# A gated cross-attention layer: query and key stages put into one block, feed-forward weights kept on chip, residual with bias formed in the query stage

## The reference, cut to what matters

```
q = layernorm(x) @ Wq + bq            # 2048 rows, 16 heads of 32
k, v = split(ctx @ Wkv + bkv)         # 4096 keys
q, k, v rounded to 8-bit steps; softmax(q k^T) rounded; out = probs @ v
x = x + tanh(g_xattn) * (out @ Wp + bp)
w1, w2 rounded to (-1, 0, 1) * mean|w|
h = layer_norm(gelu(silu(w1 . round(rmsnorm(layernorm(x))) + b1)))
x = x + tanh(g_ffn) * (w2 . round(rmsnorm(h)) + b2)
```

## Time and profile before

| | |
|---|---|
| median of the runs | 1780.82 us (1779.55 to 1785.1, 3 runs) |
| the profiled execution, its own time | 1781.48 us |
| span from its first to its last instruction | 1779.7 us |
| mean granted TensorE clock | 0.962 |
| busy: PE, DVE, ACT, POOL | 87%, 92%, 78%, 74% of the span |
| query stage, from the first instruction to the last rounding | 0 to 82 us |
| key stage, from the first transpose to the last store's issue | 91.6 to 259.7 us |
| attention begins | 262.4 us |

### The profile page before, as it was taken

One profiled execution on the slowest core, in us unless ns is written; L12 is line 12 of the kernel. 1 busy time (PEld: TensorE's weight loads), 2 busy tenths in 40 slices (PEclk: granted clock), 3 DMA queues, 4 the chain that ended last, 5 costly groups with the idle time before them and its releaser, 6 DMA issues.

```text
span 1779.7 us, 34673 instructions
## 1 busy us (share of the span) xinstructions
PE 1541.5 (87%) x13207; PEld 754.3 (42%) x13207; DVE 1636.9 (92%) x2214; ACT 1393.1 (78%) x1351; POOL 1320.5 (74%) x1297
## 2 busy tenths in 40 slices
PE   7799967898888889889898988988888887789996
PEld 4344422444444444444444444444444443333332
DVE  7869968999999999999999999999999998388987
ACT  4468867788898888889888888987888886577873
POOL 0156755899889889898988898898999898355342
PEclk9989987999999999999999999999999998799998
DMA  6769966999958999995898998688888876123223
GB/s 207 258 200 356 340 245 128 169 179 175 171 106 149 170 171 186 169 162 111 148 179 170 184 170 151 115 149 160 148 158 141 156 141 132 60 46 85 63 63 83
DMA packets 725640, 282.62 MB, mean 159 GB/s; under 512 B 676121, under 2 KB 680793, under 8 KB 724194
## 3 DMA queue, kind: packets, MB, share of 16 engines
q1 hardware_dynamic: 724098, 277.47, 75.5%
q0 software_dynamic: 704, 1.62, 0.3%
q10 hardware_dynamic: 672, 1.31, 0.2%
HBM read 76.59 MB, written 35.95 MB: 63 GB/s over the span
## 4 chain that ended last, share of the span: by engine, by line
DVE 40%; POOL 18%; PE 14%; issue 10%; ACT 2%; DMA 1%; POOLq 0%; SPq 0%; DVEq 0%; ACTq 0%
DVE att_scaled L1662 38%; POOL att_probsT L1395 14%; PE att_scores L1181 3%; PE att_scores L1121 2%; PE att_ps_o L1201 2%; PE att_scores L1141 2%; POOL att_low_row L1385 2%; PE att_scores L1182 1%; POOL att_bias_row L1388 1%; PE att_scores L1083 1%; ACT att_pairs L1261 1%; DVE att_v_largest L1631 1%; PE att_ps_v L1111 0%; ACT att_head_area L1293 0%; PE att_ps_o L1102 0%
## 5 line engine op out<-in xcount | busy, mean ns | idle before, releaser
L1662 DVE TENSOR_SCALAR_CACHE_REDUCE att_scaled<-att_scores,layer_nsq 128x1536 f32<-128x1536 f32 (+1 forms) x768 | 1202.0, 1634 | 19.7 <-PE att_scores L1141 16.6
L1261 ACT ACTIVATE att_pairs<-att_scaled,att_bias_row 128x4096 uint8<-128x4096 f32 x256 | 950.5, 3713 | 112.2 <-DMA att_pairsT<-att_pairs 76.9
L1395 POOL CAST att_probsT<-att_pairsT 128x2048 bf16<-128x2048 uint8 x512 | 953.6, 1891 | 101.9 <-DMA att_pairsT<-att_pairs 90.3
L1141 PE MATMUL att_scores<-first_head_area 96*128 96x512 bf16 x1024 | 299.3, 397 | 94.7 <-DVE att_scaled L1662 78.4
L1141 PE MATMUL att_scores<-att_head_area 96*128 96x512 bf16 x1024 | 290.2, 386 | 64.2 <-DVE att_scaled L1662 60.7
L1102 PEld LDWEIGHTS att_ps_o<-att_v_head,att_probsT 128*128 128x128 bf16 x8192 | 243.1, 96 | 65.9 <-issue 3.6
L1102 PE MATMUL att_ps_o<-att_v_head,att_probsT 128*128 128x32 bf16 x8192 | 245.3, 177 | 2.7 <-DMA att_v_head<-layer_w2T 2.6
L1141 PEld LDWEIGHTS att_scores<-first_head_area 96*128 96x128 bf16 x1024 | 81.8, 99 | 256.7 <-DVE att_scaled L1662 173.0
L1083 PE MATMUL att_scores<-att_head_area 96*128 96x512 bf16 x621 | 170.6, 384 | 0.0
L1141 PEld LDWEIGHTS att_scores<-att_head_area 96*128 96x128 bf16 x1024 | 80.0, 98 | 212.9 <-DVE att_scaled L1662 149.6
L1083 PE MATMUL att_scores<-first_head_area 96*128 96x512 bf16 x570 | 158.7, 388 | 0.0
(11 more groups left out here) (181 smaller groups left out, 1630.6 us busy)
## 6 DMA issues: line engine op xcount, KB each, us to landing
layer_w2T<-ctx_T SPq DMA_DIRECT2D x96, 256.0 KB, 3.9
k_rows<-kv_parts SPq DMA_DIRECT2D x32, 392.0 KB, 4.3
q_w_in<-in_L_ffn_w_dram SPq DMA_DIRECT2D x32, 256.0 KB, 2.8
kv_weights_ctx_in<-in_ctx_dram SPq DMA_DIRECT2D x32, 256.0 KB, 4.8
kv_weights_w_in<-in_L_ffn_w_dram SPq DMA_DIRECT2D x32, 256.0 KB, 5.1
ctx_T<-kv_inT SPq DMA_DIRECT2D x8, 1024.0 KB, 6.5
q_x_in<-in_x_dram SPq DMA_DIRECT2D x16, 256.0 KB, 3.6
terns<-kv_tern SPq DMA_DIRECT2D x32, 128.0 KB, 4.7
```

The costliest lines, as they stand in the source:

```text
L1141: last = pe.matmul(buffer[:, x:x + 512], q_head[slot][:, at:at + P], k_head[slot][:, STARTS[j] + x:STARTS[j] + x + 512], start=True, stop= ...
L1261: act.activation(pairs[g % R_BUFS][:, :].bitcast(U8).rearrange("p (c two) -> p two c", two=2), scaled[u][:, :].rearrange("p (two c) -> p t ...
L1395: pool.tensor_copy(probsT[g % C_BUFS][:, parity * HALF:(parity + 1) * HALF, :].rearrange("p k q -> p (k q)"), bytes_now.rearrange("p (n tw ...
L1662: dve.tensor_scalar(scaled[u][:, STARTS[j]:STARTS[j] + WIDTHS[j]], scores[(g * NCH + j) % 2][:, 0:WIDTHS[j]], kept["nsq"][:, g:g + 1], Non ...
```

## The change

Both projections become one function, `project`, in one block. What moves and what goes:

- **One block.** PE, ACT and DVE run `query_step(g)` for the row tiles and then `step(g)` for the context tiles, PE and ACT with the last query steps between the first three key steps. SP's `next_loads` is followed by bv, the last four `xb` stores and the last query stores; ctx tile 4 and all later loads come behind these.
- **Weights.** The 32 pieces are loaded once into 32 places of SBUF (w2T's area, a part of `o_sum`, a new area). ACT sums them as before; `round_weights(m)` rounds in place, three steps behind instead of one, in `tern` buffers that are part of `q_stage`, so the first waits for the query stores.
- **Residual with bias.** POOL adds the gated bias to each x tile that the query stage has loaded anyway (`add_bias`), into `xb` buffers in `o_sum`, and SP stores it. x's buffers are free again only after both DVE and POOL have used them. `inT` lies in the same part of `o_sum`, so ACT's first copy into it waits for all `xb` stores.
- **Gates first.** ACT issues the gate loads ahead of wq and takes the Tanh before the first square root; bp's load follows bq.
- POOL's order: bias adds with two groups of query stores between them, b1's split, the third group, then the pads and the partition sum. `wq` shares its place with the key parts.
- The last block of values is kept and its largest taken two steps earlier.

```diff
-def project_queries(nc, t, kept, next_loads):
-def project_keys_values(nc, t, kept, wk, bk, wv, bp, gates, weights_in, ...):
+def project(nc, t, kept, o_sum, next_loads, wk, bk, wv, bp, gates, weights_in, ...):
...
+        shared = c.sb("shared", [P, PART_BUFS * KEY_ROW // 2], F32)
+        wq = shared[:, 0:CT * C].rearrange("p (k n) -> p k n", n=C)
+        parts = [shared[:, i * KEY_ROW // 2:(i + 1) * KEY_ROW // 2].bitcast(BF16) for i in range(PART_BUFS)]
+        inT = [o_sum[:, i * CT * BLOCK:(i + 1) * CT * BLOCK].rearrange("p (k n) -> p k n", n=BLOCK) for i in range(2)]
+        tern = [q_stage[:, 0, i * C:(i + 1) * C] for i in range(TERN_BUFS)]
+        xb = [o_sum[:, i * C:(i + 1) * C] for i in range(XB_BUFS)]
...
+                def load_x(g):
+                    after(sp, xn_ready, g - X_BUFS + 1)
+                    after(sp, xb_ready, g - X_BUFS + 1)
+                    sp.dma_start(x_in[g % X_BUFS][:, :], x_tiles[:, g, :]).then_inc(x_loaded[g % X_BUFS], 16)
+                def load_pieces(g):
+                    after(sp, w_summed, 2 * (g - 1))
+                    for m in (2 * g, 2 * g + 1):
+                        sp.dma_start(pieces[m], tile_and_piece(t, m)[1]).then_inc(a_loaded[g % 2], 16)
...
-                        after(sp, tern_ready, n - IN_BUFS + 1)
-                        sp.dma_start(w_in[n % IN_BUFS][:, :], piece).then_inc(w_loaded[n % IN_BUFS], 16)
-                    m = g - 2
+                    m = g - ROUND_LAG - 1
...
+                for g in range(X_BUFS, QT):
+                    load_x(g)
+                    store_x(g - X_BUFS)
+                    load_pieces(g - 2)
+                for g in range(QT - 2, QT):
+                    load_pieces(g)
+                for buffer, source, sem in next_loads:
+                    sp.dma_start(buffer, source).then_inc(sem, 16)
                 sp.dma_start(kept["bv"][:, :], t["L0_xattn_bkv"][C:2 * C].rearrange("(k p) -> p k", p=P),
+                for i in range(QT - X_BUFS, QT):
+                    store_x(i)
+                store_queries(sp, 3, last_q_stored)
                 for g in range(STEPS + 1):
+                    if g == 4:
+                        sp.wait_ge(q_stored, 16 * 3 * (H // 4))
+                        sp.wait_ge(last_q_stored, 16 * (H // 4))
+                        for a in range(3):
+                            sp.dma_start(q_first[a * D:(a + 1) * D, :], t["q_ints"][0, :, :]).then_inc(q_loaded, 16)
                     step(g)
...
+                        if n < 2:
+                            pe.wait_ge(weights_in, 64)
+                            pe.wait_ge(q_math, QPER * (QT - 2 + n) + 1)
...
+                pe.wait_ge(q_const, 1)
+                for g in range(Q_FULL):
+                    query_step(g)
+                for g in range(3):
+                    step(g)
+                    query_step(Q_FULL + g)
+                for g in range(3, STEPS):
                     step(g)
...
                 def round_weights(m):
+                    if m == 0:
+                        act.wait_ge(w_math, 2)
+                        act.wait_ge(q_stored, 16 * 3 * (H // 4))
+                        act.wait_ge(last_q_stored, 16 * (H // 4))
+                    act.activation(pieces[m], pieces[m], ACT.Identity,
...
+                        if g == 0:
+                            for i in range(XB_BUFS):
+                                act.wait_ge(xb_stored[i], 16 * QT // XB_BUFS)
...
+                    if live(g - ROUND_LAG, KT - 1):
+                        round_weights(g - ROUND_LAG)
...
+                    if g - ROUND_LAG == KT - 1:
+                        round_weights(KT - 1)
+                for i, name in enumerate(("g_xattn", "g_ffn")):
+                    act.dma_start(gates[:, i:i + 1], t[name].partition_broadcast(P)).then_inc(gates_in, 16)
+                act.dma_start(wq, t["L0_xattn_Wq"].rearrange("(k p) n -> p k n", p=P)).then_inc(q_weights_in, 16)
+                act.dma_start(bq[:, :], t["L0_xattn_bq"].partition_broadcast(P)).then_inc(q_weights_in, 16)
+                act.dma_start(bp[:, :], t["L0_xattn_bp"].partition_broadcast(P)).then_inc(gated_ready, 16)
+                act.wait_ge(gates_in, 32)
+                act.activation(kept["gate_tanh"][:, :], gates[:, :], ACT.Tanh).then_inc(gates_ready, 1)
...
+                def add_bias(i):
+                    pool.wait_ge(x_loaded[i % X_BUFS], 16 * (i // X_BUFS + 1))
+                    after(pool, xb_stored[i % XB_BUFS], 16 * (i // XB_BUFS))
+                    pool.tensor_tensor(xb[i % XB_BUFS], x_in[i % X_BUFS][:, :], bp[:, :], ALU.add).then_inc(xb_ready, 1)
+                for i in range(QT):
+                    add_bias(i)
+                    if i in STORE_AT:
+                        store_queries(pool, STORE_AT.index(i), q_stored)
                 split_bias()
+                store_queries(pool, 2, q_stored)
+                pool.wait_ge(q_ready, QT)
+                pool.wait_ge(w_summed, 2 * QT)
+                for i in range(PART_BUFS):
+                    pool.memset(parts[i][:, H * HEAD_PITCH:KEY_ROW], 0.0).then_inc(pads_ready, 1)
+                pool.wait_ge(total_ready, 1)
+                pool.partition_all_reduce(total_all[:, :], total[:, :], P, RADD).then_inc(total_all_ready, 1)
```

More of the change, by code:

```diff
@@ L473, in project_keys_values @@
         q_loaded = c.sem("q_loaded")
-        xb_loaded = [c.sem(f"xb_loaded{i}") for i in range(XB_BUFS)]
         xb_stored = [c.sem(f"xb_stored{i}") for i in range(XB_BUFS)]
@@ L478, in project_keys_values, with store_queries @@
         gated_ready = c.sem("gated_ready")
-        NPER = 5
-        K_STORES = 2
+        QPER, W_LAG = 6, 2
+        NPER, K_STORES = 5, 2
         PER_BLOCK = BLOCK // P
         STEPS = KT + 5
-        XB_LOAD, XB_ADD, XB_STORE = 2, 4, 6
+        ROUND_LAG = 3
+        Q_FULL = QT + 2
+        Q_HEADS = 48
+        STORE_AT = (10, 14)
         x_tiles = t["x"].rearrange("b (i p) c -> p (b i) c", p=P)
         xb_tiles = t["xb"].rearrange("b (i p) c -> p (b i) c", p=P)
-        def row_tile(g, first):
-            i = (g - first) // 2
-            return i if (g - first) % 2 == 0 and 0 <= i < QT else None
+        sq_tiles = sq[:, :].rearrange("p (h i) -> p h i", i=QT)
+        def store_queries(eng, i, stored):
+            eng.wait_ge(q_kept, (i + 1) * QT // 4)
+            rows = slice(i * ROWS // 4, (i + 1) * ROWS // 4)
+            for g in range(H // 4):
+                eng.dma_start(t["q_ints"][4 * g:4 * g + 4, :, rows].rearrange("h d r -> (h d) r"),
+                              q_stage[:, g, rows]).then_inc(stored, 16)
         with nc.Block() as block:
@@ L582, in step @@
                             last.then_inc(v_ready, 1)
-                for g in range(STEPS):
+                pe.wait_ge(q_const, 1)
[5 more added lines that the diff above has]
+                for g in range(3, STEPS):
                     step(g)
@@ L598, in round_weights @@
                     after(act, tern_stored[m % TERN_BUFS], 16 * (m // TERN_BUFS))
-                    act.activation(tern[m % TERN_BUFS][:, :], w_in[n][:, :], ACT.Sign, bias=up_down[:, 1:2]).then_inc(tern_ready, 1)
+                    act.activation(tern[m % TERN_BUFS], pieces[m], ACT.Sign, bias=up_down[:, 1:2]).then_inc(tern_ready, 1)
                 def keep_values(j):
@@ L1755, in gated_layer @@
             ctx_in = [kv.sb(f"ctx_in{i}", [P, C], F32) for i in range(IN_BUFS)]
-            w_in = [kv.sb(f"w_in{i}", [P, C], F32) for i in range(IN_BUFS)]
             kv_loaded = kv.sem("loaded")
```

508 lines of the change are left out of this document (220 added, 288 removed).

## The result

| | before | after |
|---|---|---|
| median of the runs (five each, one chip) | 1779.55 us | 1788.39 us (1786.82 to 1790.25) |
| ratio after / before, 95% interval | | 1.0046 [1.0033, 1.0060] |
| last query products begin | 74.27 | 86.66 |
| key products of tile 0, of tile 3 | 94.29, 109.07 | 100.69, 117.28 |
| first scores of attention | 262.47 | 269.21 |

The time lies in the predicted range (1773 to 1791), 5.4 us above the point forecast of 1783. It is 8.8 us more than before, and so slower by more than the 5.3 us that count as no change: the outcome to which the prediction gave 0.29, where it gave 0.53 to no change. The time that rival 3 gave was 1793.

What follows compares the result with a forecast made beforehand. The query stage was taken as bound by DVE and PE, the key stage by PE. On 1781.5: + 4.5 (DVE held) - 2.4 (hole) - 1.0 (tail) + 1.3 (Exp table) = 1783.9, said as 1783 us; range 1773 to 1791.

Steps and rivals of the forecast that it cites:

- rival 3: Query stage: DVE pays each bias add in full, + 13.9 for + 4.5, giving 1793 us; chance 0.16.
- DVE held by the adds: Query stage: ten POOL adds each hold DVE 0.45 us, + 4.5 us, bounds 0 and 13.9.
- hole, last query products to key 3: Between query and key stage: key 3 at 106.7 for 109.07, gain 2.4 us, bounds 0 and 15.3.
- key stage, product 3 to 31: Key stage: bound by PE without stalls, so fewer loads and adds there are worth nothing.
- tail, product 31 to attention: End of key stage: k_rows leaves at 258.2 for 258.63, xb store behind it gone; 1.0 us gained, between 0 and 2.
- Exp's table load: Attention's start: Exp needs its own table after Sqrt's, + 1.3 us on the path, 0 if PE's wait has another cause.
- An add starts when its x tile lands: Query step: add starts 1.35 us after L320, ends at 2.6, so L338 is held 0.65 us.
- The feedback: Query stage: a held step makes the next add come earlier in its step; two holds sum to some 0.65 us.
- Its own range: The forecast's own range: 1779 to 1788 us, from a hold of 0.1 to 0.85, 2 us either way at the hole.
- rival 1: Hole: the clock stays up, gain 6.8 us, giving 1779, or 1774.5 with adds that hold nothing; chance 0.22.
- rival 2: Hole: xb stores land early and the block runs through, gain 15.3 us, giving 1771; chance 0.12.
- rival 4: Query stage's start: POOL's first arithmetic stalls 7.21 us, + 4.5 us, giving 1788; chance 0.08.

Runs made afterwards that it cites:

- e8: The kernel before, run again unchanged for a second profile: 1776.83 us, one run.
- e1: Kernel after with each bias add cut to 16 of 512 columns; order, waits, loads and stores stay: 1776.57 us, ratio 0.9982 to before.
- e2: Kernel after with whole adds, from the fifth on also waiting for the rounding of five tiles back: 1779.57 us, ratio 1.0000 to before.
- e3: Kernel after with eight xb buffers instead of four, so no add waits for the xb store of four tiles back: 1785.96 us, ratio 1.0032.
- e4: Kernel after with the xb buffers in the first head's area, so inT no longer waits for xb stores: 1782.86 us, ratio 1.0025 to before.
- e7: e6 with SP issuing context tiles 4 and 5 ahead of the last query stores: 1763.90 us, ratio 0.9904 to before.
- e10: Kernel after with the bias adds put back into the key stage, x tiles loaded a second time: 1774.13 us, ratio 0.9962 to before.
- e6: e5 with key weights, context tiles and value weights loaded within the query loop, key products not awaiting value weights: 1770.87 us, ratio 0.9931 to before.
- e9: e7 with the key weights loaded as four 256 KB slices from row tile 5 on: 1764.14 us, ratio 0.9914 to before.
- e11: Kernel after with POOL's two groups of query stores behind all sixteen adds: 1785.80 us, ratio 1.0038 to before.
- e5: Kernel after with the edits of e2 and e4 together: 1770.14 us, ratio 0.9928 to before.

## Why the prediction was nearly right, and which step was not

| term of the sum | forecast | measured in after |
|---|---|---|
| DVE held by the adds | + 4.5 (0 to 13.9) | + 12.4 (86.66 - 74.27) |
| hole, last query products to key 3 | - 2.4 | - 4.2 (34.80 to 30.62) |
| key stage, product 3 to 31 | 0 | 0.0 (132.03 both) |
| tail, product 31 to attention | - 1.0 | - 1.5 (21.37 to 19.90) |
| Exp's table load | + 1.3 | 0 |

The first four give + 6.7, and attention began 6.74 later. The two profiled spans differ by 8.7, the medians by 8.8: the other 2 us lie behind the start of attention, where e8 and the first profile of the same kernel differ by 2.3.

**The step that failed** is the size of the hold, and in it the sentence "An add starts when its x tile lands", 1.35 us after L320. The mechanism and its place were right (L338 to L359, exempt what reads PSUM, rival 3's point of decision at a mean hold of 0.75; measured 12.4 over ten steps, 1.24). But these are the waits of POOL in after, us in total, times, longest:

```profile
POOL layer_o_sum L585 <- DMA xb<-layer_o_sum: 29.7, 10, 5.2
```

Ten adds start only when the xb store of four tiles back has landed, and SP issues that store 0.4 us behind the x tile's load:

```profile
40.09 0.38 SPq L303 DMA_DIRECT2D pre_x_in<-in_x_dram  x1
40.52 0.43 SPq L312 DMA_DIRECT2D xb<-layer_o_sum  x1
...
44.77 1.26 POOL L585 TENSOR_TENSOR layer_o_sum<-pre_x_in,layer_bp 128x512 f32<-128x512 f32 x1 [3.67 <-DMA xb<-layer_o_sum]
```

In the four steps from 27 to 48 us the adds begin 1.85 to 2.55 us after L627, about where the part that can be held begins (1.97), and each holds it for 0.97 to 1.05 us. The two that come sooner (1.60 and 1.17) hold 0.75 and 0.31. The wait stands in the diff (`after(pool, xb_stored[i % XB_BUFS], ...)`); the prediction's walk has no such wait, and priced the stores at 0.12 us a step, as what makes landings later. e1 shows the price of the adds (11.8 us), e2 that the moment alone decides it (8.8 with whole adds), e3 that the store's landing is only part of the lateness.

The feedback on which the prediction counted is there: the load and the store of 40.09 and 40.52 go out while L651 is held (39.92), so that the longer step brings the next add sooner in its own. In e1, where nothing is held, the same four adds begin 2.92 to 3.65 us after the bias add, in after 0.8 to 1.6 us sooner. By the prediction's working, from a start at 1.35, that halves the hold; from where the adds really start it doesn't take them out of the part that is held.

Rival 3 is what happened, with six holds near its price and two of twice that. Above their usual lengths the eight held instructions add 9.7 us. Two shorter holds (0.92 and 0.48 us for 0.17, at 56.18 and 61.08) add 1.1, and 0.74 is a wait of DVE for PE at 63.94: PE had been idle for 2.57 us, its granted clock was 0.50 from 58 to 60, and eight matmuls took 4.92 us. The last 0.9 I haven't placed.

**Luck.** The range held, but not by the sum. Its own range allowed a hold of 0.1 to 0.85 us. With 12.4 for 4.5 and the other terms as forecast it would have given 1791.8, less the 0.7 between profile and median 1791.1, just outside. Hole, tail and table load each came out better than forecast, 3.6 us together, and the range had been stretched into rival 3.

**The hole**: right in its cause and order. Key 0 began 14.0 us after the last query products (forecast some 13), behind the xb stores on SP's queue, over 6 us long at half the clock; context tile 4 made PE wait 1.72. The rows of after:

```profile
87.52 5.84 SPq L312 DMA_DIRECT2D xb<-layer_o_sum  x4
...
100.69 6.18 PE L426 MATMUL pre_ps_k<-kv_weights_wk,layer_o_sum 128*128 128x512 f32 x8 [7.90 <-ACT layer_o_sum L509]
...
116.79 0.66 PE L412 MATMUL pre_ps_in<-layer_ident,kv_weights_ctx_in 128*128 128x128 f32 x4 [1.72 <-DMA kv_weights_ctx_in<-in_ctx_dram]
```

e4 and e7 take the two waits away one by one. Key product 1 began 6.7 us after product 0 where I had priced 8.1, as the clock came back earlier (0.57 from 104 to 106, 1.00 from 106 to 108), and PE's wait for context tile 4 was 1.72 for some 3; so the gain was 4.2.

**Fewer loads and adds in the key stage: nothing.** Right, by the 132.03 us of before, after and e10 from key product 3 to 31.

**The Exp's table load** cost nothing. It didn't stand behind the wait for POOL's row but ran under it. Rows of after:

```profile
273.90 1.28 ACT L1258 ACT_TABLE_LOAD   x1
276.27 3.71 ACT L1258 ACTIVATE att_pairs<-att_scaled,att_bias_row 128x4096 uint8<-128x4096 f32 x1 [1.08 <-POOL att_bias_row L1385]
```

The Exp begins 7.06 us after attention's start, 7.05 in before; ACT's idle time ahead of it is 1.08 instead of 2.38. Neither the load's 1.28 nor the 2.66 of the Trainium skill ("ScalarE: Activation LUTs", "What ACT_TABLE_LOAD costs") came onto the path.

**Rivals 1, 2 and 4** didn't come: the granted clock was 0.50 from 96 to 104; the xb stores landed last; POOL's first arithmetic at 11.82 had no gap but its data's.

**Left open**: why e4 and e6 changed the length of the query stage; why the x tile of the long step in e6, e7 and e9 (6.9, 6.2, 5.9 us) landed so late; what in attention, whose lines are the same in all fourteen profiles, makes it last from 1508 to 1522 us to the end of the span. No run was made on these.

## What to carry to other kernels

Work moved to an idle engine beside a full one must be timed, not only placed: find which instructions of the full engine it shuts out, and release it by a semaphore at the point of the step from which none of them runs for as long as it lasts. When a forecast hangs on the moment at which an instruction starts, write down every wait ahead of it in the diff and take the one that ends last: here it was the store of four tiles back, not the load. And a transfer that a critical tile stands behind in the queue may be part of that tile's latency: issue it behind the tile where that is possible. Slices alone cured nothing in e9.

## What the runs showed of the hardware that was not expected

- Four DMA issues on POOL (2.48 and 2.16 us) directly ahead of an add: the DVE instruction begun before the add (0.84 and 0.56 us) lasted 2.41 us, until after the add's end. Twice in after, and in e4 2.42 and 2.08 us; without the pair (e11) none was over 1.5. Issues alone (e2, e5) hold nothing, and the pair holds nothing where the add falls on the first instructions of a step (e2, e5). Why the hold begins before the add does, no run here shows.
- The table load for the first Exp was carried out while ACT waited for POOL's row: 1.28 us, and the Exp began no later after attention's start.
- An x tile of 256 KB issued 0.54 us behind 1 MB landed after 9.9 us (e9), for 3.4 in before; one issued 0.53 us behind 256 KB took 7.6 in the same run, so the size ahead isn't shown to be what counts.
